# A chunked recurrence on one core: the order of convolution taps, products and value stores within a chunk

## What is computed

```python
q = _causal_dwconv_silu(x @ Wq.T, qcw, qcb).reshape(Bb, Tt, H, DK)
k = _causal_dwconv_silu(x @ Wk.T, kcw, kcb).reshape(Bb, Tt, H, DK) * SCALE
v = _causal_dwconv_silu(x @ Wv.T, vcw, vcb).reshape(Bb, Tt, H, DV)
a = jax.nn.sigmoid(x @ Wa.T + ba).reshape(Bb, Tt, H, DV)
beta = jax.nn.sigmoid(x @ Wb.T + bb)

def step(S, inp):
    qt, kt, vt, at, bt = inp
    err = jnp.einsum('bhij,bhj->bhi', S, kt) - vt
    S = at[..., None] * S - bt[..., None, None] * (err[..., None] * kt[:, :, None, :])
    o = jnp.einsum('bhij,bhj->bhi', S, qt)
    return (S, o)
```

## Time and profile before

| | us |
|---|---|
| median of 3 runs | 7076.88 |
| lowest, highest | 7072.87, 7079.59 |
| profiled execution | 7082.73 |
| span of its instructions | 7080.9 |

### The profile page before, as it was taken

The page is one execution under the profiler, slowest core; times in us unless marked ns, Lnnn a source line. Parts: engine busy times, 40 slices in busy tenths (PEclk is TensorE's granted clock), DMA queues, the critical chain, the costliest instruction groups (busy, mean ns, idle before and its releaser), DMA issues. The chain is left out here.

```text
span 7080.9 us, 176655 instructions
## 1 busy us (share of the span) xinstructions
PE 5011.9 (71%) x58695; PEld 3311.0 (47%) x58695; DVE 5420.1 (77%) x15973; ACT 3320.2 (47%) x7234; POOL 3639.8 (51%) x4232
## 2 busy tenths in 40 slices
PE   5666766666667666667666626888888888888877
PEld 4555555455555555555555523344444444444433
DVE  5889888888898888888888855666666666666665
ACT  4554455445544554455444513444444444444444
POOL 3778777877787778787877761111111111111110
PEclk8877777787777778787777757888888888888888
DMA  4666666666666666666666641111111111111111
GB/s 121 164 159 163 168 164 155 168 167 165 155 168 169 160 158 167 167 167 157 164 168 159 161 123 42 45 45 45 48 45 45 45 45 45 45 45 45 47 45 36
DMA packets 1197390, 804.68 MB, mean 114 GB/s; under 512 B 1049827, under 2 KB 1101699, under 8 KB 1188484
## 3 DMA queue, kind: packets, MB, share of 16 engines
q1 hardware_dynamic: 1134212, 610.21, 36.1%
q10 hardware_dynamic: 62464, 185.09, 8.2%
HBM read 490.57 MB, written 304.55 MB: 112 GB/s over the span
## 5 line engine op out<-in xcount | busy, mean ns | idle before, releaser
L469 POOL TENSOR_TENSOR qp<-qp,ab 128x512 f32<-128x512 f32 (+7 forms) x1024 | 980.0, 957 | 75.3
L474 POOL TENSOR_TENSOR qp<-qp,pt 128x512 f32<-128x512 f32 (+7 forms) x1024 | 961.6, 939 | 80.2
L1778 DVE TENSOR_REDUCE nmax<-w_bank 128x1 f32<-128x512 f32 x1024 | 643.0, 684 | 405.7 <-PE w_bank L1360 401.3
L851 DVE SCALAR_TENSOR_TENSOR p_bank<-y,conv_w,p_bank 128x128 f32<-128x128 f32 x3072 | 825.5, 347 | 50.7 <-ACT p_bank L668 22.8
L1315 POOL TENSOR_TENSOR ot<-ot,ln_w 128x1024 f32<-128x1024 f32 x64 | 150.7, 2355 | 1143.2 <-ACT ot L1617 1143.2
L535 PE MATMUL d_bank<-st 64*32 64x80 f32 x16384 | 493.5, 289 | 340.6 <-issue 315.0
L471 POOL TENSOR_TENSOR pt<-qp,vb 128x512 f32<-128x512 f32 (+7 forms) x1024 | 724.3, 707 | 11.4 <-DVE vb L928 9.3
L507 PE MATMUL d_bank<-xd,kt 32*64 32x128 f32 x7936 | 354.7, 328 | 455.9 <-DVE st L869 392.1
L1320 POOL TENSOR_TENSOR x1b<-x,bias 128x256 f32<-128x256 f32 x64 | 46.3, 723 | 1165.7 <-DVE bst L1874 1165.7
L599 PEld LDWEIGHTS p_bank<-xnT,wqkv 128*128 128x128 f32 x4096 | 548.4, 216 | 187.6 <-issue 187.6
L599 PE MATMUL p_bank<-xnT,wqkv 128*128 128x128 f32 x4096 | 597.1, 306 | 43.1 <-ACT st L681 34.9
(11 more groups left out here) (219 smaller groups left out, 11656.1 us busy)
## 6 DMA issues: line engine op xcount, KB each, us to landing
db<-decay_dram SPq DMA_DIRECT2D x124, 1024.0 KB, 12.3
prod_dram<-prod ACTq DMA_DIRECT2D x128, 640.0 KB, 7.9
kp<-prod_dram SPq DMA_DIRECT2D x512, 80.0 KB, 2.6
qp<-prod_dram SPq DMA_DIRECT2D x256, 160.0 KB, 2.9
a_dram<-at ACTq DMA_DIRECT2D x64, 512.0 KB
ab<-a_dram SPq DMA_DIRECT2D x64, 512.0 KB, 5.8
v_dram<-vt ACTq DMA_DIRECT2D x64, 512.0 KB
vb<-v_dram SPq DMA_DIRECT2D x64, 512.0 KB, 5.7
```

What stands on the lines that cost most here:

```text
L469: link(nc.gpsimd.tensor_tensor(q, q, ab[:, g, r:r + 1, :].to_broadcast([128, w, DV]), ALU.mult), 1)
L474: link(nc.gpsimd.tensor_tensor(q, q, pt2[:, 0:w], ALU.add))
L851: nc.vector.scalar_tensor_tensor(out=zz, in0=y[:, j % Y_BANKS, i, :, tap:tap + C], scalar=conv_w[:, m, tap:tap + 1], in1=zz, op0=ALU.mult, ...
L1778: nc.vector.tensor_reduce(nmax[:, n:n + 1], bank[:], AX.X, ALU.max, negate=True).then_inc(freed, 1)
```

## The change

- VectorE: six groups of taps stand ahead of the first half instead of nine, twelve between the halves instead of nine. The state additions stand behind groups 6, 8, 12 and 14 instead of 9, 12, 14 and 16.
- TensorE: the projection of bank 5 moves from ahead of the second update to behind the third; projection 0 of the chunk after moves behind the fourth; `products` stands between projections 0 and 1 of the chunk after, and all four value and key transposes behind projection 1. `products` waits for the placed keys instead of silu 4.
- ScalarE: silu 2 moves behind the gates, which are stored at once, ahead of `crossed`; eviction 5 moves behind the placing of the keys; the product copies stand ahead of silu 5, of the eviction of bank 1 and of the value copies.
- SyncE: the sums are loaded in two parts with a semaphore each (VectorE waits for the first in its second half, GpSimd for the second); the load of `vb` moves behind the first keys' loads.

```diff
-STATE_AFTER_TAPS = (9, 12, 14, 16)
+EARLY_TAPS = 2 * (TAPS - 1)
+STATE_AFTER_TAPS = (6, 8, 12, 14)
@@ SyncE
-                    sp.dma_start(xk[:], x_dram[g].rearrange("t b h i -> (b h) t i")).then_inc(xk_in[g], 16)
+                    sums = x_dram[g].rearrange("t b h i -> (b h) t i")
+                    sp.dma_start(xk[:, 0:HALF], sums[:, 0:HALF]).then_inc(xk_in[g], 16)
+                    sp.dma_start(xk[:, HALF:C], sums[:, HALF:C]).then_inc(xq_in[g], 16)
...
-                if valid(lo + 1, hi + 1):
-                    sp.wait_ge(*dma_of(v_wr, n, g, 1))
-                    held(sp, sp_passed)
-                    sp.dma_start(vb[:, o], v_dram[o].rearrange("t b h i -> (b h) t i")).then_inc(vb_in[o], 16)
...
                     for h in range(4):
                         sp.dma_start(kp[h:128:4, 0:HALF], rows[h, 0, :, 0:HALF]).then_inc(kp_in[o], 16)
+                    sp.wait_ge(*dma_of(v_wr, n, g, 1))
+                    held(sp, sp_passed)
+                    sp.dma_start(vb[:, o], v_dram[o].rearrange("t b h i -> (b h) t i")).then_inc(vb_in[o], 16)
@@ GpSimd
-                        pool.wait_ge(*dma_of(xk_in, n, g, 0))
+                        pool.wait_ge(*dma_of(xq_in, n, g, 0))
@@ TensorE, products
-                pe.wait_ge(silu_done, CONV_BANKS * s + 5)
+                pe.wait_ge(keys_placed, s + 1)
@@ TensorE, slot
                 if state:
                     update(*before, (0,))
-                if front:
-                    project(s + 1, 1 - g, 5)
                 if ahead:
                     betas(s + 2, g)
...
                 if state:
                     update(*before, (2,))
-                if ahead:
-                    project(s + 2, g, 0)
+                if front:
+                    project(s + 1, 1 - g, 5)
                 if state:
                     update(*before, (3,))
                 if ahead:
+                    project(s + 2, g, 0)
+                if front:
+                    products(s + 1, n + g, 1 - g)
+                if ahead:
                     project(s + 2, g, 1)
                 if front:
-                    front2(s + 1, n + g, 1 - g, (0, 1))
-                    products(s + 1, n + g, 1 - g)
-                    front2(s + 1, n + g, 1 - g, (2, 3))
+                    front2(s + 1, n + g, 1 - g, range(4))
@@ ScalarE, crossed
                     act.wait_ge(*dma_of(xk_in, n, g, -2))
+                    act.wait_ge(*dma_of(xq_in, n, g, -2))
@@ ScalarE, slot
                 if front:
-                    for j in range(3):
+                    for j in range(2):
                         silu(s + 1, 1 - g, j)
-                        if j < 2:
-                            evict(s + 1, 1 - g, j + 3)
+                        evict(s + 1, 1 - g, j + 3)
                 if ahead:
                     gates(s + 2, n + 1, g)
                     betas(s + 2, n + 1, g)
-                if front:
-                    evict(s + 1, 1 - g, 5)
-                    silu(s + 1, 1 - g, 3)
-                    place_keys(s + 1, 1 - g)
-                if valid(lo, hi):
-                    crossed(s, n, g)
-                if ahead:
                     store_gates(s + 2, n + 1, g)
                     store_betas(s + 2, n + 1, g)
                 if front:
+                    silu(s + 1, 1 - g, 2)
+                if valid(lo, hi):
+                    crossed(s, n, g)
+                if front:
+                    silu(s + 1, 1 - g, 3)
+                    place_keys(s + 1, 1 - g)
+                    evict(s + 1, 1 - g, 5)
                     silu(s + 1, 1 - g, 4)
                 if ahead:
-                    for j in range(2):
-                        evict(s + 2, g, j)
+                    evict(s + 2, g, 0)
                 if front:
+                    products(s + 1, n + g, 1 - g)
                     silu(s + 1, 1 - g, 5)
+                if ahead:
+                    evict(s + 2, g, 1)
+                if front:
                     values(s + 1, n + g, 1 - g)
-                    products(s + 1, n + g, 1 - g)
                     key_rows(s + 1, 1 - g)
@@ VectorE, slot
-                    for k in range(TAP_GROUPS // 2):
+                    for k in range(EARLY_TAPS):
                         conv(s + 1, k)
...
-                groups = iter(range(TAP_GROUPS // 2, TAP_GROUPS))
+                groups = iter(range(EARLY_TAPS, TAP_GROUPS))
```

More of the change, by code:

```diff
@@ L259, in layer0_recurrence @@
         values_scaled, cross_done = sem("values_scaled"), sem("cross_done")
-        e_wr, xe_in, x_wr, xk_in = ([sem(f"{name}{g}") for g in range(GROUPS)] for name in ("e_wr", "xe_in", "x_wr", "xk_in"))
+        e_wr, xe_in, x_wr, xk_in, xq_in = ([sem(f"{name}{g}") for g in range(GROUPS)] for name in ("e_wr", "xe_in", "x_wr", "xk_in", "xq_in"))
         kl_in = [sem(f"kl_in{g}") for g in range(GROUPS)]
```

## The result

The changed kernel takes 7477.64 us (median of 4 runs, 7472.05 to 7494.52) beside 7075.85 us of the kernel before: 1.0572 times, 95% interval 1.0553 to 1.0590, so 5.7% slower. The forecast was slower by 1.7%, and its range ended at 7287 us. The span of the profiled execution is 7470.2 us, 389 us more than before. What follows the recurrence takes as long as it did (2874.7 us before, 2873.3 after, from the end of the last solve to the end of the span); the loss lies in the recurrence.

A forecast was written before the change was run, and what follows sets the result against it. VectorE's slot, with its wait for `xk`, and GpSimd 1.7 us behind bound the kernel. Late values would add 2.0 us over some 60 slots, +120 us: 7203, less 5.8 for the median, 7197 us; range 7000 to 7287.

The forecast's parts named there:

- the two margins: GpSimd's scaling 1.7 us ahead of VectorE's first half, the `vb` load some 4.6 us ahead of GpSimd; these decide.
- The wait for `xk`: VectorE's wait for the sums ahead of its second half, 3.9 us in the slot, falls under 1 us a slot.
- The new wait of VectorE and that of GpSimd: VectorE waits some 6 us a slot for scaling ahead of its first half, GpSimd 4 to 5 for `vb`.
- The products' start condition: TensorE's products may start once the fourth pair of state additions, behind the ninth group, is done, at 2007.1.
- +2.0 us a slot: `vb` lands late, so VectorE's first half starts at 2039.8 instead of 2037.80.
- The last step of the recorded sum: GpSimd's scaling: `vb` landed at 2037.7, plus 1.9 us, given as 2039.7.
- The gate store beside the load of `xe`: Late `xe` delays TensorE's cross products 0 to 1 us; 0.3 taken, swallowed by the margin just won.
- The pause kept at its length: TensorE's pause within the products, beside the `db` load, stays 4.15 us, so product copies end at 2021.1.
- rival (c): TensorE's pause in the products grows under the `db` load, copies end at 2024: +4.9 us a slot, 7370 us; chance 0.08.
- From the last copy to the store: Bank 1's projection and eviction, then two value copies, put the value store at 2026.5, 5.4 us after the copies.
- The two transfers: The values' way through DRAM: store 5.8 us, then load of `vb` 5.4 us, 11.2 us together.
- rival (a): Values come in time and GpSimd sets the slot, some -2.1 us a slot, 6951 us; chance 0.2.

The follow-up runs named there:

- Experiment 2: Changed kernel with value transposes, copies, store and load back ahead of the products; taps, split load and early gate store as changed: 7071.56 us, 0.9989 of the kernel before.
- experiment 5: Changed kernel with VectorE's part undone (nine groups of taps ahead, nine between, additions behind 9, 12, 14, 16): 7467.59 us, 1.0542 of the kernel before.
- experiment 1: Changed kernel with the stores of gates and betas put back behind the copies and stores of the sums on ScalarE: 7349.29 us, 1.0374 of the kernel before.
- Experiment 6: Changed kernel with the second 1 MB broadcast of `db` cut to one row, orders kept: 7248.82 us, 1.0229 of the kernel before.
- Experiment 10: Experiment 1 with value transposes ahead of bank 1's projection and value copies and store ahead of its eviction, still behind the products: 7205.55 us, 1.0178.
- experiment 3: Changed kernel with values first and the stores of gates and betas behind the sums: 7122.20 us, 1.0055 of the kernel before.
- experiments 11 and 12: Kernel before with the split load of the sums alone: 7020.74 us; then also with stores of gates and betas behind the key copies: 6967.42 us.

## Why the prediction was wrong

**Right: what decides.** The prediction named the two margins, 1.7 us of GpSimd and 4.6 us of `vb`, and said that the delayed values would use them up. Experiment 2 shows it: with the values back in place the loss is gone. The wait for `xk` went as forecast. The new wait of VectorE and that of GpSimd came where they were forecast, but longer: 10.0 us instead of some 6, and 7.6 instead of 4 to 5. And experiment 5 bears out that VectorE waits out what it wins by the taps. The products' start condition, nine groups and four pairs, was right as well: with the gate store out of the way (experiment 1) they begin 21.0 us behind the first half, beside the sum's 2007.1 - 1986.2 = 20.9 behind the decay.

**Wrong: the size, +2.0 us a slot against 6.9 in the slot shown.** The value store was forecast 40.3 us behind the decay and came at 45.6. (The last step of the recorded sum, 2037.7 + 1.9, is 2039.6 and not 2039.7; that changes nothing here.) By the steps of the sum:
- *The gate store beside the load of `xe`, priced at 0 to 1 us and swallowed.* It cost 3.5 us in this slot (cross products at 13.2 instead of 9.7), and the products start 2.5 us behind the forecast; their first copy, forecast 2 us sooner, came 0.5 us later than before. Experiment 1 gives it back: 128 us, some 2.1 us a slot. The failed step was twofold: the price, taken with no row of two such transfers together, and that a margin swallows it. The margin was that of the sums' way; the products, and so the values, hang on the cross products too. The trace shows how narrow the place is. In 4 of the 34 slots the gate store is issued 3.3 us or more behind the errors' store, and the cross products wait for `xe` for 1.0 us at most. In 17 it is issued 1.4 to 2.6 us behind, and they wait 1.8 to 4.1 us. In 13 it is issued 0.4 to 1.8 us ahead, and they wait 3.9 to 5.5 us.
- *The pause kept at its length, 4.15 us.* It is 6.38 us in the slot shown, 6.5 in the mean: 1.4 us more by the last copy. This was rival (c) in mechanism, at half of its price. Experiment 6 shows that the `db` transfers are behind it.
- *From the last copy to the store, 5.4 us.* It was 2068.83 - 2062.08 = 6.75. The projection behind the products took 3.64 us, not 2.05. The granted clock was lower: the stretch behind the pause, as the second of these two shows (columns as in the heading, clock after GpSimd's busy time), has a granted clock of 0.53, near the lower of the two levels (1.2 of 2.4 GHz), and the whole projection now falls into it.

```profile
core 0: us, PE busy (x) PEld busy (x) DVE busy (x) ACT busy (x) POOL busy (x), PEclk, DMA share, GB/s
2042.00:2052.00 10.00, 8.09 (x243) 7.32 (x246) 10.00 (x35) 8.17 (x22) 1.16 (x1) 1.00 0.73 171
...
2059.30:2065.20 5.90, 5.90 (x80) 5.67 (x80) 5.21 (x14) 1.48 (x4) 5.66 (x6) 0.53 0.53 211
```

The clock in the stretch before, 2042 to 2052 us, was 1.00, and TensorE had stood idle for 6.4 us between. In the kernel before, the stretch behind the pause (2019.5 to 2024.2 us, granted clock 0.50) held the rest of the products and the keys' transposes, and the projection of bank 1 was long done (2.05 us at 2003.98). Experiment 10, which takes the projection and an eviction off the path, gains 144 us.
- *The two transfers, 5.8 and 5.4 us.* They took 6.5 and 4.3 us (2068.83 to 2075.29, and from there to 2079.5), together 10.7 instead of 11.2. This term held.

So 2.5 + 1.4 + 1.35 = 5.25 us late at the store, less 0.5 for the transfers, on top of the 2.0 forecast: 6.8 us, against 6.9 read off the slot. The chances had the right sign, 0.63 for slower. The range ended at +3.5 us a slot, so it left 1.5 us for all that might come on top of the 2.0, and the first of these terms alone took more.

The fit of the Trainium skill, "DMA: Bandwidth & Descriptors", section "Anatomy of one DMA — SWDGE (gpsimd) path", which spoke for rival (a), is given there for GpSimd's kind of queue. It doesn't carry over to the queues of this case: the estimate of 6.4 us for the two transfers stands against 10.7 measured.

**Not settled:** how the 50 us of experiment 3 divide between GpSimd's wait and the longer pause, and by what way the `db` transfers delay the instruction packets behind which TensorE goes on.

## What to carry to other kernels

When a wait is filled by moving work, list what waited beside it with less margin than the wait was long; here GpSimd had 1.7 us and the values' load 4.6, and moving the values by 16 us couldn't fit. Price each DMA that changes place by what it will run beside, on every chain that hangs on the delayed transfer, and not only on the one that won a margin. And try the parts alone: on the kernel before, the split load and the gate store moved the other way gain 1.6%, while the change as a whole, with the same split load in it, lost 5.7.

## What the runs showed of the hardware

- A store slows loads on another queue by much: two loads of 256 KB landed in 6.3 us with a 512 KB store of another queue in flight and in 3.6 without it (experiments 11 and 12). In experiments 2 and 3 the same loads landed in 3.9 and 6.2 us.
- A large store can hold back a small one that is issued behind it on another queue. In the changed kernel, in the 13 of 34 slots in which the gate store of 512 KB was issued 0.4 to 1.8 us ahead of the errors' store of 256 KB, this one landed after 6.2 to 7.5 us. In the 21 slots in which it was issued 1.4 us or more behind, the errors' store landed after 2.3 to 3.2 us, as in experiment 1 (2.3 to 3.4), where the gate store is far away. The border isn't sharp: in experiment 2 one errors' store took 7.9 us with the gate store 0.9 us behind it. One of the 13 slots, in which the load of `xe` can only be issued 6.66 us behind its store:

```profile
2237.09 0.60 ACTq L771 DMA_DIRECT2D a_dram<-at  x1
```

```profile
2238.40 0.38 SPq L343 DMA_DIRECT2D e_dram<-eb  x1
2245.06 0.66 SPq L348 DMA_DIRECT2D vt<-e_dram  x1
```

The Trainium skill, "DMA: Bandwidth & Descriptors", section "Queues, rings and completion order", says that a completion is written only after every earlier write of that DMA engine, across its queues. The late landing in the 13 slots agrees with it, but the runs can't tell this from plain sharing.
- Two broadcasts of 1 MB make TensorE pause for 5 to 6.5 us in the middle of a dense run of small matmuls, with nothing that it waits for in the profile; with half of the load the pause is 4.0 us. With the load moved away it is 0.5 us a slot there (19.1 / 36), and 1.7 us a slot (59.5 / 36) turn up in the work beside which the load then runs. The pauses end 2.4 to 3.2 us behind the start of a 16 KB instruction packet, 35 of 35 in the changed kernel.
- Such a pause costs twice: the stretch behind it ran at a granted clock of 0.53, and a projection in it took 3.64 instead of 2.05 us.
